# Folding the adjacency matrix over neighbouring 1024-column blocks instead of over its two halves

## The chip, the cores and the metric

The kernel runs on one core of a Trainium2 chip. The core has a TensorE (PE), a VectorE (DVE), a ScalarE (ACT), a GpSimd (POOL) and a SyncE (SP), and 16 DMA engines that all transfers share. The metric is device time in microseconds of one execution; the kernel before has a median of 1272.74 us over three runs (1272.05 to 1274.66).

## The reference

For x (8192 x 512) and adj (8192 x 8192, float32, sparse: about nine positive entries in a row, the diagonal always one of them):

```python
h = maximum(layernorm(x), 0)
mask = adj > 0
head = mask / maximum(sqrt(sum(mask * mask, -1)), 1e-12)
inc = adj + head                      # head is one value per row, at its nonzeros
out = x + (inc @ h) / sum(inc, -1)
```

## The kernel before, in words

The product is not done densely. For each row the kernel finds the nonzero entries and their columns, gathers those rows of h, and sums them with weights.

**Layer norm.** Sixteen chunks of 512 rows of x are loaded (L376), normed by DVE and ACT, and stored to a scratch tensor h in HBM (L380). A lane (partition) holds four rows in a run, so each lane's part of such a transfer is one run of 8 KB. ACT waits for the constants that POOL sets up (L466 to L491, one instruction after the other, each waited for) before its first piece of work (L732).

**Tiles.** There are 64 tiles of 128 rows, tile t being row t % 4 of each lane's four rows of chunk t // 4. The matrix rows of a tile are 4 MB. They come in four chunks of 1 MB (`load_chunk`, L382 to L391, queue of SP) into one of two buffers, `A[:, t % 2]`. A chunk j holds 1024 columns of the left half of the matrix and 1024 of the right half, the first beginning at 1024 j, the second at 4096 + 1024 j. In HBM these are two runs of 4 KB per lane, 16 KB apart; in SBUF they lie side by side, 8 KB.

**Fold.** For tiles 0 to 60 (`FOLDED` = 61) `fold` (L767) computes right * 2^100 + left into one row of 1024 words, on DVE. The entry tells by its size from which side it came. MAX8 (L794) and FIND_INDEX8 (L798) then take the eight greatest words and their places: 32 candidates in a row from four chunks. Where both sides have an entry in one column of a fold, or a chunk has over eight entries, the row is "bad". `check` on ACT (L564 to L575, four passes over 2048 words for each tile) and the list in `count_bad` (L1022) find such rows; up to 128 of them are done again in an extra tile, the batch (number 64), with no fold. In the matrix of the reference's inputs 51 rows of tiles 0 to 60 are bad with the fold over halves and 49 with the fold over neighbours (counted in that matrix; both are under 128, so the dense loop behind the batch, L433, is not entered). Tiles 61 to 63 and the batch are "wide": eight parts of 1024 columns, MAX8 and FIND_INDEX8 on each, no fold.

**Gather and product.** The two greatest of each chunk are a row's own entries, 8 slots; the rest spill, and the tile's spilled entries share 3 x 128 places (4 x 128 in the wide tiles). POOL gathers h rows of 2 KB with indirect DMAs, eight and three in a tile (`gather_own` L499, `gather_spill` L507); ACT builds diagonal matrices of the weights, and PE multiplies and sums them (L1326, L1337). Empty places name no row, so they move no data.

**Order.** Each engine has its order of work written out, in periods. In period t DVE does the four folds of tile t with the small work of tiles t - 1, t - 2 and t - 3 between them. SP, in period t, issues chunks 0 and 1 of tile t + 2, the store of tile t - 4 (L400, waits for ACT's copy), for t >= 16 the load of x for the residual (L396, waits for `own_done`, PE's own product of tile t - 2), and then chunks 2 and 3. A chunk's load waits until tile t has been checked by ACT and folded by DVE, and, if the diagonal of the tile lies in it (`diag_chunk`), until the diagonal has been read. So a chunk is asked for nearly two periods before it is folded.

**Names that the change touches.** `diag_half` and `diag_chunk` (L208, L211), `part` (L250), `load_chunk` (L391), the constants `base_own` and `base_spill` (L485, L487), `part_columns` to `part_places` (L801 to L818), `columns_any` (L862) and `count_bad` (L1028 to L1037).

Of the kernel before, what the change touches and what calls it, by code (L numbers as in the profile page):

```python
# [4 lines left out]
P = 128  # L5


def add_graph_layer(nc, x, adj, out):
# [14 lines left out]
    CHUNKS = 4  # L23
# [46 lines left out]
    adj_h = adj.rearrange("(c p j) (h n) -> c j p h n", p=P, j=ROWS, h=2)  # L70
# [3 lines left out]
    with ctx:  # L74
# [76 lines left out]
        right_diag = sb("right_diagonal_sign", [P, FOLDED - TILES // 2], fp32)  # L151
# [56 lines left out]
        def diag_half(t):  # L208
            return t // ROWS * P * ROWS // HALF

        def diag_chunk(t):  # L211
            return t // ROWS * P * ROWS % HALF // CW
# [36 lines left out]

        def part(i):  # L250
            return i % 2 * CHUNKS + i // 2
# [110 lines left out]
        def turn(t):  # L362
            return t // 2 + 1
# [8 lines left out]
        def _(sp):  # L372
# [9 lines left out]
            def load_chunk(t, j):  # L382
                if t >= 2:
                    sp.wait_ge(checked, 4 * (t - 2) + 2 * (j // 2) + 2)
                    if wide(t - 2):
                        sp.wait_ge(idx_found, searched(t - 2) + 2 * j + 2)
                    else:
                        sp.wait_ge(folded, CHUNKS * (t - 2) + j + 1)
                        if j == diag_chunk(t - 2):
                            sp.wait_ge(diag_read, t - 1)  # L390
                sp.dma_start(chunk(t % 2, j), adj_h[t // ROWS, t % ROWS, :, :, CW * j:CW * (j + 1)]).then_inc(adj_loaded[t % 2][j], 16)  # L391
# [58 lines left out]
        def _(pool):  # L450
# [19 lines left out]
            step(nc.gpsimd.memset(on_diag[:, FOLDED:BATCH + 1], 0.0))  # L470
            step(nc.gpsimd.memset(ones[:], 1.0))
# [13 lines left out]
            count_up(base_own[:, 0], [[0, 2], [CW, CHUNKS]], int(SKIP), 0)  # L485
            count_up(base_own[:, 1], [[CW, PARTS]], int(SKIP), 0)
            count_up(base_spill[:], [[0, 6], [-CW, CHUNKS]], 0, 0)  # L487
# [260 lines left out]
        def _(dve):  # L748
# [52 lines left out]
            def part_columns(t, i):  # L801
                if t == BATCH:
                    return A[:, 0, CW * part(i):CW * (part(i) + 1)]
                return chunk(t % 2, part(i) % CHUNKS)[:, part(i) // CHUNKS]

            def part_values(t, i):
                if t == BATCH:
                    dve.wait_ge(batch_adj, 16)
                else:
                    dve.wait_ge(adj_loaded[t % 2][part(i) % CHUNKS], 16 * turn(t))  # L810
                e = slice(8 * part(i), 8 * part(i) + 8)
                nc.vector.max(out=cv[:, t % 2, e], in_=part_columns(t, i)).then_inc(vals_found, 1)  # L812

            def part_places(t, i):
                dve.wait_ge(vals_found, searched(t) + i + 1)
                e = slice(8 * part(i), 8 * part(i) + 8)
                nc.vector.max_index(out=ci[:, t % 2, e], in_max=cv[:, t % 2, e],  # L817
                                    in_values=part_columns(t, i)).then_inc(idx_found, 1)  # L818
# [43 lines left out]
            def columns_any(t):  # L862
                dve.wait_ge(halves_told, t + 1)
                dve.wait_ge(idx_found, searched(t) + searches(t))
                nc.vector.scalar_tensor_tensor(out=ranked(cola[:], t), in0=ranked(ge[:], t), scalar=float(HALF),
# [156 lines left out]
            def count_bad():  # L1022
# [5 lines left out]
                on_right = slice(TILES // 2, FOLDED)  # L1028
                step(nc.vector.tensor_scalar(right_diag[:], on_diag[:, on_right], LEAST, None, ALU.is_ge))
                step(nc.vector.tensor_tensor(well[:], cnt_all[:, every], right_all[:, every], ALU.subtract))  # L1030
                step(nc.vector.tensor_tensor(well[:, on_right], well[:, on_right], right_diag[:], ALU.subtract))
# [4 lines left out]
                step(nc.vector.scalar_tensor_tensor(out=z_right[:, on_right], in0=right_diag[:], scalar=ZERO,  # L1036
                                                    in1=z_right[:, on_right], op0=ALU.mult, op1=ALU.add))  # L1037
# [415 lines left out]
```

## Time and profile before

| | |
|---|---|
| median of the runs | 1272.74 us (1272.05 to 1274.66) |
| profiled execution, span | 1276.7 us |
| DMA packets, MB | 148207, 471.00 |
| queue of SP (q1): packets, MB, share of 16 engines | 90368, 331.38, 66.3% |
| queue of POOL (q0): packets, MB, share of 16 engines | 57744, 138.64, 29.7% |
| adjacency chunks of 1 MB | 256 |

The span goes from the first to the last instruction of one profiled execution; its time is 4.0 us above the median of the runs, and no other time of that execution is given. A share of 16 engines is the time that packets took over 16 times the stretch; it can pass 100% a little, since packets overlap. "Remote" as a releaser means that the profile does not know it, and "issue" that the engine waited for nothing that the profile shows.

### The profile page before, as it was taken

Reading aid. Unit: us, or ns where it says so; the run is one execution under the profiler, and the core shown is the slowest. Engines: PE = TensorE matmul, PEld = TensorE weight load, DVE = VectorE, ACT = ScalarE, POOL = GpSimd, SP = SyncE. Lnnn points to the kernel's source line nnn. Section 1 sums busy time; section 2 is a strip of 40 time slices with the busy share of each in tenths; the row PEclk is TensorE's granted clock in tenths of the full one; section 3 lists DMA queues with packets and bytes.
Section 4 is the critical chain, followed back from the end, with each engine's and each line's share of the span. In section 5 each row is a group of like instructions: output and inputs, shape, how many; then the busy total and the mean of one; then the engine's idle time right before and its main releaser. Section 6 shows DMA issues by size and latency. Waiting matters only on the chain.

```text
span 1276.7 us, 14660 instructions
## 1 busy us (share of the span) xinstructions
PE 959.0 (75%) x2680; PEld 478.1 (37%) x2682; DVE 1189.2 (93%) x2868; ACT 975.5 (76%) x1902; POOL 791.1 (62%) x748
## 2 busy tenths in 40 slices
PE   0003878888888878787988887978878888977677
PEld 0001434444444444443434443434444434433343
DVE  6679999998999999998999999999999999999961
ACT  6657787887887988786888877888877888884731
POOL 1003667676666777776766767777776776765562
PEclk9999899898988989899898989999989988987888
DMA  9999999999999999999999999999999999997532
GB/s 356 427 422 406 396 394 388 369 387 369 379 378 382 401 373 401 395 401 394 402 400 401 392 374 384 399 400 395 402 396 402 402 397 373 401 390 275 175 106 74
DMA packets 148207, 471.00 MB, mean 369 GB/s; under 512 B 24826, under 2 KB 24826, under 8 KB 143965
## 3 DMA queue, kind: packets, MB, share of 16 engines
q1 hardware_dynamic: 90368, 331.38, 66.3%
q0 software_dynamic: 57744, 138.64, 29.7%
q8 instruction: 25, 0.41, 0.1%
q14 instruction: 70, 0.57, 0.1%
HBM read 490.47 MB, written 33.82 MB: 411 GB/s over the span
## 4 chain that ended last, share of the span: by engine, by line
DVE 55%; issue 17%; DMA 11%; ACT 6%; PE 6%; another core or an unknown queue 2%; SPq 1%; POOL 0%; DVEq 0%; ACTq 0%; POOLq 0%
DVE cand_word L794 17%; DVE folded L772 16%; DMA adj_tile<-in_adj_dram 8%; DVE cand_index L798 6%; DMA gathered_rows<-in_x_dram 3%; PE acc L1326 3%; DVE cand_index L817 2%; DVE cand_word L812 2%; ACT junk L573 2%; ACT adj_tile L560 2%; ACT diag L636 1%; PE acc L1337 1%; DVE diagonal_alone L779 1%; DVE entry L961 1%
## 5 line engine op out<-in xcount | busy, mean ns | idle before, releaser
L494 POOL DMA_INDIRECT gathered_rows<-h_scratch,slot_column x520 | 559.9, 1077 | 263.1 <-issue 158.0
L573 ACT ACTIVATE junk<-adj_tile,zero_unit 128x2048 bf16<-128x2048 f32 x256 | 510.0, 1998 | 48.3 <-issue 27.5
L1326 PE MATMUL acc<-gathered_rows,diag 128*128 128x512 f32 x1040 | 489.6, 622 | 21.4 <-DMA gathered_rows<-h_scratch,slot_column 18.2
L494 POOL DMA_INDIRECT gathered_rows<-h_scratch,spill_column x198 | 223.1, 1127 | 195.0 <-ACT spill_column L619 135.2
L794 DVE MAX8 cand_word<-folded 128x8 f32<-128x1024 f32 x244 | 298.2, 1222 | 5.9 <-remote 1.3
L772 DVE SCALAR_TENSOR_TENSOR folded<-adj_tile 128x1024 f32<-128x1024 f32 x244 | 296.1, 1214 | 7.7 <-DMA adj_tile<-in_adj_dram 5.6
L1326 PEld LDWEIGHTS acc<-gathered_rows,diag 128*128 128x128 f32 x1040 | 203.8, 204 | 263.4 <-issue 262.6
L798 DVE FIND_INDEX8 cand_index<-cand_word,folded 128x8 uint32<-128x1024 f32 x244 | 297.3, 1219 | 0.0
L1337 PE MATMUL acc<-gathered_rows,spill_matrix 128*128 128x512 f32 x396 | 186.8, 609 | 46.0 <-DMA gathered_rows<-h_scratch,spill_column 42.4
L636 ACT ACTIVATE diag<-ident,weights_and_payload 128x128 f32<-128x128 f32 x581 | 176.2, 388 | 16.0 <-issue 6.5
L1337 PEld LDWEIGHTS acc<-gathered_rows,spill_matrix 128*128 128x128 f32 x396 | 72.8, 192 | 154.8 <-issue 154.6
L1320 PE MATMUL acc<-own_row,diag 128*128 128x512 f32 x122 | 78.0, 726 | 68.6 <-ACT own_row L646 60.6
L1276 PE MATMUL poff<-spill_rank,lanes_before 128*128 128x1 f32 x130 | 22.7, 244 | 119.4 <-DVE spill_rank L859 116.8
L1299 PE MATMUL pbrought<-weights_and_payload,owner 128*128 128x72 f32 (+1 forms) x384 | 73.2, 340 | 30.8 <-DVE weights_and_payload L919 16.2
L1276 PEld LDWEIGHTS poff<-spill_rank,lanes_before 128*128 128x128 f32 x130 | 27.8, 226 | 163.5 <-issue 140.0
L611 ACT ACTIVATE owner<-powner,last_lane_half 128x384 f32<-128x384 f32 (+1 forms) x65 | 37.4, 575 | 58.1 <-remote 44.2
L1305 PE MATMUL pturned<-ident,owner 128*128 128x128 f32 x396 | 78.2, 350 | 0.6
L1299 PEld LDWEIGHTS pbrought<-weights_and_payload,owner 128*128 128x128 f32 x384 | 63.6, 243 | 33.2 <-issue 20.7
L1305 PEld LDWEIGHTS pturned<-ident,owner 128*128 128x128 f32 x396 | 67.4, 250 | 3.3 <-ACT spill_matrix L627 1.4
L646 ACT ACTIVATE own_row<-x_residual,ln_bias,ln_rstd 128x512 f32<-128x512 f32 x45 | 36.1, 802 | 38.0 <-remote 37.5
L1320 PEld LDWEIGHTS acc<-own_row,diag 128*128 128x128 f32 x122 | 23.6, 216 | 108.2 <-issue 91.8
L627 ACT ACTIVATE spill_matrix<-pturned,entry 128x128 f32<-128x128 f32 x198 | 57.1, 361 | 1.1 <-PE acc L1337 1.1
(151 smaller groups left out, 880.1 us busy)
## 6 DMA issues: line engine op xcount, KB each, us to landing
adj_tile<-in_adj_dram SPq DMA_DIRECT2D x256, 1024.0 KB
h_scratch<-adj_tile SPq DMA_DIRECT2D x16, 1024.0 KB, 10.6
out_dram<-out_tile SPq DMA_DIRECT2D x64, 256.0 KB
gathered_rows<-in_x_dram SPq DMA_DIRECT2D x12, 1024.0 KB, 12.6
x_residual<-in_x_dram SPq DMA_DIRECT2D x48, 256.0 KB
gathered_rows<-h_scratch,slot_column POOLq DMA_INDIRECT x520
x_held<-in_x_dram SPq DMA_DIRECT2D x4, 1024.0 KB, 7.9
gathered_rows<-h_scratch,spill_column POOLq DMA_INDIRECT x198, 3.5
```

The source lines that it names most:

```text
L494: nc.gpsimd.indirect_dma_start(out=into, out_offset=None, in_=h[:, :], in_offset=bass.IndirectOffsetOnAxis(ap=column, axis=0), bounds_chec ...
L573: nc.scalar.activation(junk[:, n % 2].rearrange("p (j c) -> p j c", j=2), both[:, :, half], ACT.Relu, bias=zero_unit[:], scale=-UP, accum_ ...
L627: last = nc.scalar.activation(W[:, t % 2, g], pturned[:, g * P:(g + 1) * P], ACT.Copy, scale=entry[:, t % 2, g, 0:1])
L636: last = nc.scalar.activation(diag[:, t % 2, s], ident[:], ACT.Copy, scale=wpay[:, t % 2, s:s + 1])
L772: nc.vector.scalar_tensor_tensor(out=F[:, j % 2], in0=a[:, 1], scalar=UP, in1=a[:, 0], op0=ALU.mult, op1=ALU.add).then_inc(folded, 1)
L794: nc.vector.max(out=cv[:, t % 2, 8 * j:8 * j + 8], in_=F[:, j % 2]).then_inc(vals_found, 1)
L798: nc.vector.max_index(out=ci[:, t % 2, 8 * j:8 * j + 8], in_max=cv[:, t % 2, 8 * j:8 * j + 8], in_values=F[:, j % 2]).then_inc(idx_found, 1)
L1299: last = nc.tensor.matmul(bank[:, c:c + 3 * n], owner[:, g * P:(g + 1) * P], wpay[:, t % 2, 1 + OWN:1 + OWN + 3 * n], start=True, stop=True)
L1305: last = nc.tensor.matmul(pturned[:, g * P:(g + 1) * P], owner[:, g * P:(g + 1) * P], ident[:], start=True, stop=True)
L1320: nc.tensor.matmul(acc[t % 3][:], diag[:, t % 2, 0], again[:], start=False, stop=False)
L1326: last = nc.tensor.matmul(acc[t % 3][:], diag[:, t % 2, 1 + s], slot(t % 2, s), start=False, stop=False)
L1337: last = nc.tensor.matmul(acc[t % 3][:], W[:, t % 2, g], slot(t % 2, OWN + g), start=False, stop=(g == groups(t) - 1))
```

## The change

A chunk is now 2048 columns in a row: columns 2048 j to 2048 j + 2047, of which the right 1024 are folded onto the left 1024. The load of a lane is one run of 8 KB. Bytes, chunks, folds, and the layout in SBUF within a chunk (left, right) are the same. The rest follows from that: which chunk and which side hold the diagonal, the columns' bases, and the wide tiles' parts, which now stand in order of the columns. Since the diagonal now is on the right side in every second group of eight tiles and not in tiles 32 to 60, POOL sets up a row of marks, `on_right`, with two more memsets, and `count_bad` works with all 61 tiles where it took 29.

```diff
-    adj_h = adj.rearrange("(c p j) (h n) -> c j p h n", p=P, j=ROWS, h=2)
+    adj_t = adj.rearrange("(c p j) n -> c j p n", p=P, j=ROWS)
...
         def diag_half(t):
-            return t // ROWS * P * ROWS // HALF
+            return t // ROWS * P * ROWS % (2 * CW) // CW
         def diag_chunk(t):
-            return t // ROWS * P * ROWS % HALF // CW
+            return t // ROWS * P * ROWS // (2 * CW)
...
-                sp.dma_start(chunk(t % 2, j), adj_h[t // ROWS, t % ROWS, :, :, CW * j:CW * (j + 1)]).then_inc(adj_loaded[t % 2][j], 16)
+                sp.dma_start(A[:, t % 2, 2 * CW * j:2 * CW * (j + 1)],
+                             adj_t[t // ROWS, t % ROWS, :, 2 * CW * j:2 * CW * (j + 1)]).then_inc(adj_loaded[t % 2][j], 16)
...
+            step(nc.gpsimd.memset(on_right[:], 0.0))
+            step(nc.gpsimd.memset(on_right[:].rearrange("p (c h k) -> p c h k", h=2, k=CW // P)[:, :, 1], 1.0))
...
-            count_up(base_own[:, 0], [[0, 2], [CW, CHUNKS]], int(SKIP), 0)
+            count_up(base_own[:, 0], [[0, 2], [2 * CW, CHUNKS]], int(SKIP), 0)
...
             def part_columns(t, i):
-                if t == BATCH:
-                    return A[:, 0, CW * part(i):CW * (part(i) + 1)]
-                return chunk(t % 2, part(i) % CHUNKS)[:, part(i) // CHUNKS]
+                return A[:, t % 2, CW * i:CW * (i + 1)]
...
-                nc.vector.scalar_tensor_tensor(out=ranked(cola[:], t), in0=ranked(ge[:], t), scalar=float(HALF),
+                nc.vector.scalar_tensor_tensor(out=ranked(cola[:], t), in0=ranked(ge[:], t), scalar=float(CW),
...
-                step(nc.vector.tensor_scalar(right_diag[:], on_diag[:, on_right], LEAST, None, ALU.is_ge))
+                step(nc.vector.scalar_tensor_tensor(out=bad_rank[:], in0=on_diag[:, every], scalar=LEAST,
+                                                    in1=on_right[:, every], op0=ALU.is_ge, op1=ALU.mult))
...
-                step(nc.vector.tensor_tensor(well[:, on_right], well[:, on_right], right_diag[:], ALU.subtract))
+                step(nc.vector.tensor_tensor(well[:], well[:], bad_rank[:], ALU.subtract))
...
-                step(nc.vector.scalar_tensor_tensor(out=z_right[:, on_right], in0=right_diag[:], scalar=ZERO,
-                                                    in1=z_right[:, on_right], op0=ALU.mult, op1=ALU.add))
+                step(nc.vector.scalar_tensor_tensor(out=z_right[:], in0=bad_rank[:], scalar=ZERO,
+                                                    in1=z_right[:], op0=ALU.mult, op1=ALU.add))
```

## Rows read from the trace of the kernel before

**Rows 1.** The page: busy time by engine, and the DMA engines' tenths in 40 slices.

```profile
PE 959.0 (75%) x2680; PEld 478.1 (37%) x2682; DVE 1189.2 (93%) x2868; ACT 975.5 (76%) x1902; POOL 791.1 (62%) x748
...
DMA  9999999999999999999999999999999999997532
```

**Rows 2.** Windows: PE, PEld, DVE, ACT, POOL busy, clock, DMA share, GB/s.

```profile
0.00:20.00 20.00, 0.00 (x0) 0.00 (x0) 12.62 (x43) 12.20 (x19) 5.02 (x27) 1.00 0.85 313
100.00:200.00 100.00, 73.34 (x192) 36.87 (x193) 99.59 (x231) 81.39 (x152) 60.87 (x56) 0.93 1.02 395
...
1000.00:1100.00 100.00, 85.77 (x238) 42.98 (x239) 97.24 (x230) 79.79 (x157) 71.48 (x64) 0.90 1.02 391
```

**Rows 3.** Timeline of VectorE, two folds of a first chunk (start, us, instruction).

```profile
198.87 1.22 DVE L772 SCALAR_TENSOR_TENSOR folded<-adj_tile 128x1024 f32<-128x1024 f32 x1
...
215.87 1.22 DVE L772 SCALAR_TENSOR_TENSOR folded<-adj_tile 128x1024 f32<-128x1024 f32 x1
```

**Rows 4.** Waits of VectorE to 98.5 us (waited for: total us, times, longest).

```profile
DVE folded L772 <- DMA adj_tile<-in_adj_dram: 3.3, 3, 1.2
```

**Rows 5.** Waits of VectorE, 98.5 to 900 us.

```profile
DVE entry_value L833 <- remote: 3.3, 2, 1.7
...
DVE cand_word L794 <- remote: 1.3, 1, 1.3
```

**Rows 6.** Waits of VectorE, 900 to 1110 us.

```profile
DVE folded L772 <- DMA adj_tile<-in_adj_dram: 2.2, 4, 0.8
DVE folded L772 <- issue: 2.1, 2, 1.4
```

**Rows 7.** DMA queues, 20 to 60 us (packets, MB, share of 16 engines).

```profile
DMA packets 2353, 17.12 MB, mean 428 GB/s; under 512 B 263, under 2 KB 263, under 8 KB 263
...
q1 hardware_dynamic: 2351, 17.11, 101.3%
```

**Rows 8.** DMA queues, 84 to 96 us.

```profile
DMA packets 1039, 5.07 MB, mean 422 GB/s; under 512 B 77, under 2 KB 77, under 8 KB 764
...
q1 hardware_dynamic: 1039, 5.07, 101.5%
```

**Rows 9.** DMA queues, 400 to 900 us.

```profile
q1 hardware_dynamic: 39509, 135.50, 69.6%
q0 software_dynamic: 25431, 60.68, 32.2%
```

**Rows 10.** Chain that ended last (start us, us, what).

```profile
82.49 15.74 DMA adj_tile<-in_adj_dram
...
1011.32 2.21 SPq L396
...
1021.02 25.63 DMA adj_tile<-in_adj_dram
```

**Rows 11.** Chain that ended last, the first 10 us.

```profile
2.37 0.11 POOL ones L471
2.52 0.11 POOL zero_unit L472
...
7.53 0.21 ACT place_plus_half L732
...
9.70 2.93 ACT adj_tile L560 x4
```

**Rows 12.** Timeline of VectorE, list of bad rows.

```profile
1159.51 0.19 DVE L1031 TENSOR_TENSOR tests_passed<-tests_passed,right_diagonal_sign 128x29 f32<-128x29 f32 x1
1159.73 0.22 DVE L1032 SCALAR_TENSOR_TENSOR zeros_left<-tests_passed,zeros_left 128x61 f32<-128x61 f32 x1
```

**Rows 13.** Waits of TensorE, whole span.

```profile
PE acc L1337 <- DMA gathered_rows<-h_scratch,spill_column: 42.4, 29, 2.9
PE acc L1326 <- DMA gathered_rows<-h_scratch,slot_column: 18.2, 18, 2.3
```

**Rows 14.** Timeline of GpSimd, one gather.

```profile
214.52 1.00 POOL L494 DMA_INDIRECT gathered_rows<-h_scratch,slot_column  x1 [0.30 <-issue]
```

More of the change, by code:

```diff
@@ L150, in add_graph_layer @@
         well = sb("tests_passed", [P, FOLDED], fp32)
-        right_diag = sb("right_diagonal_sign", [P, FOLDED - TILES // 2], fp32)
+        on_right = sb("diagonal_on_right", [P, TILES], fp32)
         bad = sb("bad_rows", [P, FOLDED], fp32)
@@ L247, in searched @@
             return CHUNKS * min(t, FOLDED) + PARTS * max(t - FOLDED, 0)
-        def part(i):
-            return i % 2 * CHUNKS + i // 2
         def paid(t, k):
@@ L484, in _ @@
             count_up(placed[:], [[P, EXTRA]], 1, 1)
-            count_up(base_own[:, 0], [[0, 2], [CW, CHUNKS]], int(SKIP), 0)
+            count_up(base_own[:, 0], [[0, 2], [2 * CW, CHUNKS]], int(SKIP), 0)
             count_up(base_own[:, 1], [[CW, PARTS]], int(SKIP), 0)
-            count_up(base_spill[:], [[0, 6], [-CW, CHUNKS]], 0, 0)
+            count_up(base_spill[:], [[0, 6], [-2 * CW, CHUNKS]], 0, 0)
             count_up(b_base_spill[:], [[0, 7], [-CW, PARTS]], 0, 0)
@@ L809, in part_values @@
                 else:
-                    dve.wait_ge(adj_loaded[t % 2][part(i) % CHUNKS], 16 * turn(t))
-                e = slice(8 * part(i), 8 * part(i) + 8)
+                    dve.wait_ge(adj_loaded[t % 2][i // 2], 16 * turn(t))
+                e = slice(8 * i, 8 * i + 8)
                 nc.vector.max(out=cv[:, t % 2, e], in_=part_columns(t, i)).then_inc(vals_found, 1)
@@ L815, in part_places @@
                 dve.wait_ge(vals_found, searched(t) + i + 1)
-                e = slice(8 * part(i), 8 * part(i) + 8)
+                e = slice(8 * i, 8 * i + 8)
                 nc.vector.max_index(out=ci[:, t % 2, e], in_max=cv[:, t % 2, e],
@@ L1026, in count_bad @@
                 step(nc.vector.tensor_tensor(z_right[:], q_all[:, every, 1], q_all[:, every, 3], ALU.add))
-                on_right = slice(TILES // 2, FOLDED)
-                step(nc.vector.tensor_scalar(right_diag[:], on_diag[:, on_right], LEAST, None, ALU.is_ge))
+                step(nc.vector.scalar_tensor_tensor(out=bad_rank[:], in0=on_diag[:, every], scalar=LEAST,
+                                                    in1=on_right[:, every], op0=ALU.is_ge, op1=ALU.mult))
                 step(nc.vector.tensor_tensor(well[:], cnt_all[:, every], right_all[:, every], ALU.subtract))
-                step(nc.vector.tensor_tensor(well[:, on_right], well[:, on_right], right_diag[:], ALU.subtract))
+                step(nc.vector.tensor_tensor(well[:], well[:], bad_rank[:], ALU.subtract))
                 step(nc.vector.scalar_tensor_tensor(out=z_left[:], in0=well[:], scalar=ZERO, in1=z_left[:],
```

## The prediction

> **What bounds the kernel now.** I read the busy shares first, then the windows, the waits of VectorE, the DMA queues, and last the chain. VectorE is busy 93% of the span, ahead of ScalarE with 76% and TensorE with 75% [rows 1]. The windows sharpen that: from 100 to 200 us VectorE works 99.59 of 100 us, from 1000 to 1100 us 97.24 [rows 2]. The reader should see in the same rows that the DMA share is 1.02 in both, where 1.013 is what a stretch of nothing but queued transfers shows [rows 7]. So two resources are full. A tile costs VectorE 17.00 us (from 198.87 to 215.87, the first folds of two tiles in a row) [rows 3], and the DMA engines need about as long for the same tile. Which is the slower one is told by who waits. Ahead of the fold VectorE waits 3.3 us until 98.5 us, when the pipeline fills [rows 4]; from 900 to 1110 us 2.2 + 2.1 = 4.3 us [rows 6]; and never between: what it waits for there is no transfer [rows 5]. The second row of group 6 has "issue" as releaser; but the fold has only two conditions, the load and a search two chunks back on its own engine, so I take it as a late load too. The transfers are falling behind: a chunk landed 15.74 us after its issue at 82 us, and 25.63 us after it at 1021 us, where the chain runs through such transfers [rows 10]. VectorE is the bound of the first 50 tiles, the DMA engines by a hair that of the last ten folded ones.
>
> **The load, the part that matters.** All 64 tiles x 4 chunks x 128 lanes x 2 runs = 65536 runs of 4 KB become 32768 of 8 KB. What a run costs comes from two stretches. From 20 to 60 us there are 2351 - 263 = 2088 packets of 8 KB on the queue of SP in 1.013 x 40 x 16 = 648.3 us of engine time: 0.3105 us each, the 263 small ones counted at nothing [rows 7]; it also shows that a run of 8 KB goes as one packet. From 84 to 96 us there are 1039 - 764 = 275 packets of 8 KB and 764 - 77 = 687 of 4 KB in 1.015 x 12 x 16 = 194.9 us: (194.9 - 275 x 0.3105) / 687 = 0.1594 us for one of 4 KB [rows 8]. Two of those are 0.3188, so a joined run saves 0.0083 us of one DMA engine. Over 16 engines that is 128 x 0.0083 / 16 = 0.066 us for a chunk, 0.27 us for a tile, 17.0 us over the run. The rounding of the shares leaves about 0.0005 us on the 0.0083, or 1 us on the 17.
>
> Most of the 17 us buys nothing, because VectorE needs its 17.00 us for a tile whatever the transfers do. In the middle it only makes loads land earlier. What it can take from the time is the wait ahead of folds:
> - From 900 to 1110 us: by tile 52 the transfers have 52 x 0.27 = 14 us more in hand, over three times the 4.3 us that is lost there. I take all of it: -4.3 us. Bounds: 0 (the loads are late for another reason, below) and -4.3.
> - To 98.5 us: here the DMA engines are the bound, and stay it. Five chunks stand ahead of the fold at 98.26 us, 5 x 0.066 = 0.33: -0.3 us.
> - After 1110 us no fold or search waits for a load. The drain is a chain of gathers and products; it keeps its length and moves with VectorE.
>
> By the Trainium skill ("DMA: Bandwidth & Descriptors", section "Why small descriptors are slow (HBM only)") the fixed part of a packet is about 3 cycles, on a fabric that the same page puts at 850 MHz. An estimate from that page is 3.5 ns a packet, 32768 x 3.5 / 16 = 7.2 us over the run, where the rows gave 17.0. Even so the 52 tiles would bring 5.8 us, over the 4.3 us needed, and the sum would be the same but for 0.2 us at the start.
>
> **The small edits.** Two memsets on POOL stand in the chain of constants that ScalarE waits for before the layer norm. Such a step takes 2.52 - 2.37 = 0.15 us with its wait, and the chain of the first 10 us runs over POOL and into ScalarE's L732 with nothing between [rows 11]; the DMA engines have room then, the share is 0.85 [rows 2]: +0.3 us. The second memset is strided; nothing here shows one, and I bound it by 0 and by one more step of 0.15. In `count_bad` three operations grow from 29 to 61 elements. Of 29 they take 0.18 to 0.19, of 61 0.22 [rows 12]: 3 x 0.04, +0.1 us, on VectorE's path. The tiles whose diagonal gates a load are 16, 16, 16 and 13 for chunks 0 to 3, as before; only which ones they are differs. Diagonal reads, searches and `columns_any` have the same shapes. ScalarE's checks read the same words of SBUF.
>
> **Sum.** -4.3 - 0.3 + 0.3 + 0.1 = -4.2 us on the span of 1276.7 us: 1272.5. The profiled execution is 4.0 us above the median of the runs, and I carry the difference over: 1272.7 - 4.2 = 1268.5 us, 0.33% faster.
>
> **Rivals.**
> 1. *The loads are late because SP asks late.* SP issues chunks 2 and 3 behind a load of x that waits for TensorE's own product; the chain passes exactly there, SP L396 at 1011.32 us and then a transfer of 25.63 us [rows 10]. If the order of SP's queue decides, the 4.3 us stays and the time is 1272.7 - 0.3 + 0.4 = 1272.8 us. Against it: the long part of that chain is the transfer, which is 10 us longer than at 82 us. To this belongs also that the loads are cut in pieces of 4 KB all the same; against that stand the 8 KB packets of [rows 7]. 27%.
> 2. *More is won.* VectorE lost 3.3 + 1.3 us on waits with no known releaser between 98 and 900 us [rows 5], while transfers went on and caught up. If those belong to the profiled execution, the runs had 4.6 us more lateness of transfers, and all of it goes: 1268.5 - 4.6 = 1263.9 us. For it: the DMA share has no hole. Against: nothing shows the two kinds of execution side by side. 12%.
> 3. *The gathers are starved; slower.* The DMA engines serve two queues that are both never empty. A tile's gathers move 60.68 MB / (500 / 17.0) = 2.06 MB [rows 9], 504 pieces of 4 KB if rows go in pairs, 31.5 for each engine, 2.9 for each of eleven gathers. If the engine takes turns by packets, a gather takes 2.9 x (0.159 + 0.159) = 0.92 us now, under the 1.00 + 0.30 us at which POOL issues them [rows 14]; behind 8 KB packets it takes 2.9 x (0.159 + 0.3105) = 1.36 us, over it. The eight own gathers then end 0.44 + 8 x 0.06 = 0.9 us later, the three spilled ones 0.6 us: 1.5 us a tile for TensorE, which waits for gathers already, 60.6 us in all [rows 13]. It is idle (100 - 85.77) x 17 / 100 = 2.4 us a tile [rows 2], so this is hidden unless it stands in the chain gather, own product, load of x, chunks 2 and 3 [rows 10]. From the point where it does, say the eight tiles 52 to 59, it costs 8 x 1.5 = 12 us and the 4.3 is not won: 1272.8 + 12 = 1285 us. 13%.
>
> That taking of turns is what the Trainium skill states ("DMA: Bandwidth & Descriptors", section "Queues, rings and completion order"): an engine goes round its queues packet by packet. It is the rule that speaks against this change. No row here shows an engine's turns; what rival 3 counts with are the durations of the rows.
>
> **How the numbers follow.** The forecast has 48%, rival 1 27%, rival 2 12%, rival 3 13%. A measurement of this kernel tells 0.2%, 2.5 us, from no change. The forecast is beyond that by 1.7 us, rival 2 well beyond, rival 1 within: faster 60%, within 27%, slower 13%. The range takes in rivals 1 and 2 with a margin and leaves most of rival 3 out: 1261 to 1275 us. The forecast's own range is 1267 to 1271.
>
> **What would show it.** Packets on the queue of SP fall by 32768 to about 57600 with the same MB, and its share of the engines by 17.0 / 1276.7 = 1.3 points. The fold's waits from 900 to 1110 us are gone, those to 98.5 us still about 3. Chunks land some 10 us or more sooner after their issue late in the run. VectorE's tile stays at 17.00 us. TensorE's waits for gathers stay near 60 us; if they double and folds wait again, rival 3 holds. If the packets fall and the waits at the end remain, it is rival 1, and the step that failed is the one that gives the transfers' rate the lateness.

## The result: 0.4% slower, with late gathers in the place of late loads

The changed kernel takes 1278.38 us (median of 4 runs, 1276.44 to 1279.47), the kernel before 1273.40 us beside it (4 runs, 1272.05 to 1274.66): a ratio of 1.0042, 95% interval 1.0027 to 1.0057. The forecast was 1268.5 us, with a range to 1275. The profiled execution has a span of 1274.6 us; it belongs to the fastest of the four runs, so its waits are on the small side, while the profiled execution of the kernel before lies 4.0 us above its median. This pair of profiles shows what changed in kind and not the loss itself: from the first fold to the last, VectorE stands still for 11.0 us in the changed kernel and for 15.7 us in the kernel before (stops over 0.25 us, added up from the two traces). A run counts in a ratio if it is within 1.5% of the fastest of its kernel; that left out one of six runs of `small_owner_first` (1623 us) and two of six of `split_lanes`, and no other.

First the page of the changed kernel: span, busy shares, the DMA totals with the two queues (packets, MB, share of 16 engines), and the chain that ended last by engine.

```profile
span 1274.6 us, 14664 instructions
...
PE 939.1 (74%) x2682; PEld 451.2 (35%) x2682; DVE 1189.8 (93%) x2868; ACT 972.5 (76%) x1902; POOL 803.8 (63%) x750
...
DMA packets 115439, 470.98 MB, mean 370 GB/s; under 512 B 24824, under 2 KB 24824, under 8 KB 78431
...
q1 hardware_dynamic: 57600, 331.38, 65.3%
q0 software_dynamic: 57744, 138.62, 29.7%
...
DMA 23%; issue 21%; DVE 21%; PE 15%; POOL 9%; ACT 7%; another core or an unknown queue 1%; POOLq 1%; ACTq 0%; SPq 0%; DVEq 0%
```

VectorE's busy time is what it was [rows 1]. The queue of SP has 57600 packets, 32768 fewer, for the same 331.38 MB. The chain is another one: DMA, TensorE and GpSimd make up 23 + 15 + 9 = 47% of it and VectorE 21%, where before the three made up 11 + 6 + 0 = 17% and VectorE 55%.

From 84 to 96 us all loads are now 8 KB (columns as in [rows 8]):

```profile
DMA packets 704, 5.11 MB, mean 426 GB/s; under 512 B 80, under 2 KB 80, under 8 KB 80
...
q1 hardware_dynamic: 704, 5.11, 101.0%
```

1.010 x 12 x 16 = 193.9 us for 704 - 80 = 624 packets is 0.3108 us each, the price that [rows 7] gave.

VectorE's waits over the whole span (total us, times, longest), against [rows 4 to 6]:

```profile
DVE weights_and_payload L917 <- ACT half_minus_offset L597: 7.1, 9, 2.5
...
DVE folded L772 <- DMA adj_tile<-in_adj_dram: 3.6, 3, 1.3
DVE weights_and_payload L917 <- issue: 3.5, 7, 1.7
```

The fold's wait for loads is 3.6 us in all, and the three stops behind it are those of the filling, until 99 us; the 4.3 us of [rows 6] are gone. In their place stand 7.1 + 3.5 = 10.6 us ahead of L917, the payload of places, which needs ScalarE's `half_minus_offset`. Of these, 8.0 us lie between 98.5 and 1110 us, where the kernel before has none; the rest comes behind 1110 us, where it has 2.6 us too. TensorE's waits for gathered rows, against [rows 13]:

```profile
PE acc L1324 <- DMA gathered_rows<-h_scratch,slot_column: 61.2, 33, 3.8
PE acc L1335 <- DMA gathered_rows<-h_scratch,spill_column: 56.9, 31, 3.4
```

These are 118.1 us, where they were 60.6. With the stops that have no releaser shown, TensorE is idle ahead of these two products for 176.9 us, where it was 67.2. That second measure is the one used below to compare kernels, since profiles differ in how many stops they can name. And ScalarE's copy of the owners waits. It did so in the kernel before too, 57.7 us in all, of which 2.9 us are put down to TensorE by name and the rest so:

```profile
ACT owner L611 <- remote: 44.2, 17, 8.7
ACT owner L611 <- issue: 10.6, 8, 2.9
```

In the changed kernel it is 152.1 us in all, most of it by name:

```profile
ACT owner L611 <- PE powner L1282: 123.8, 42, 8.5
```

What ties the three together is seen in the chain that ended last, here from 297 us on (start, us, what):

```profile
297.55 9.09 DMA gathered_rows<-h_scratch,spill_column
...
306.78 5.46 PE acc L1335 x6
312.24 0.33 PE powner L1282
...
313.08 0.20 ACT spill_column L619
...
314.04 0.33 POOL gathered_rows L494
...
316.70 7.43 DMA gathered_rows<-h_scratch,spill_column
...
325.02 4.27 PE acc L1335 x6
329.29 0.44 PE powner L1282
...
333.81 7.53 DMA gathered_rows<-h_scratch,spill_column
```

Read it as a loop. The spilled rows of one tile land 9.09 us after the step ahead of them, TensorE makes their product (L1335), only then finds the owners of a younger tile (L1282), ScalarE copies these and, next in its order, converts a third tile's spill columns (L619), GpSimd issues its gathers (L494), and the loop is at the landing of the next tile's rows: 316.70 to 333.81 is 17.11 us a turn, the turn before it (297.55 to 316.70) 19.15. VectorE's tile takes 17.00 [rows 3]. The loop has become as long as VectorE's own or longer, and VectorE, which needs one turn of it for each tile, stands ahead of L917. The kernel before has the same loop in its code, but none of the 195 longest pieces of its chain is a transfer of gathered rows of h.

The constants' chain at the start, against [rows 11]:

```profile
7.95 0.21 ACT place_plus_half L732
...
10.12 2.23 ACT adj_tile L560 x3
```

L732 starts at 7.95 us where it started at 7.53, and the first layer norm at 10.12 where it was 9.70: the two memsets cost 0.4 us.

### The profile page after: what moved, and what is told of

Read it like the earlier page. It is cut to its first block, busy times and chain, and to the rows that moved or that the text cites. A ratio compares the mean times of both kernels' runs of the same rounds, so it can differ in the third digit from the quotient of the medians.

```text
span 1274.6 us, 14664 instructions
## 1 busy us (share of the span) xinstructions
PE 939.1 (74%) x2682; PEld 451.2 (35%) x2682; DVE 1189.8 (93%) x2868; ACT 972.5 (76%) x1902; POOL 803.8 (63%) x750
## 3 DMA queue, kind: packets, MB, share of 16 engines
q1 hardware_dynamic: 57600, 331.38, 65.3%
## 4 chain that ended last, share of the span: by engine, by line
DMA 23%; issue 21%; DVE 21%; PE 15%; POOL 9%; ACT 7%; another core or an unknown queue 1%; POOLq 1%; ACTq 0%; SPq 0%; DVEq 0%
DMA gathered_rows<-h_scratch,spill_column 13%; POOL gathered_rows L494 9%; PE acc L1335 8%; DMA gathered_rows<-h_scratch,slot_column 6%; PE acc L1324 5%; DVE cand_word L794 5%; DVE folded L772 5%; DMA gathered_rows<-in_x_dram 3%; ACT junk L573 3%; DVE cand_index L815 2%; DVE cand_word L810 2%; DVE cand_index L798 2%; ACT adj_tile L560 2%; DMA adj_tile<-in_adj_dram 1%; ACT diag L636 1%
## 5 line engine op out<-in xcount | busy, mean ns | idle before, releaser
L494 POOL DMA_INDIRECT gathered_rows<-h_scratch,slot_column x520 | 578.9, 1113 | 262.9 <-issue 157.8
L1324 PE MATMUL acc<-gathered_rows,diag 128*128 128x512 f32 x1040 | 501.1, 629 | 80.4 <-DMA gathered_rows<-h_scratch,slot_column 61.2
L494 POOL DMA_INDIRECT gathered_rows<-h_scratch,spill_column x198 | 216.6, 1094 | 180.1 <-ACT spill_column L619 126.0
L1335 PE MATMUL acc<-gathered_rows,spill_matrix 128*128 128x512 f32 x396 | 207.7, 667 | 96.9 <-DMA gathered_rows<-h_scratch,spill_column 56.9
L1335 PEld LDWEIGHTS acc<-gathered_rows,spill_matrix 128*128 128x128 f32 x396 | 78.0, 209 | 221.0 <-issue 221.0
L611 ACT ACTIVATE owner<-powner,last_lane_half 128x384 f32<-128x384 f32 (+1 forms) x65 | 38.0, 584 | 152.1 <-PE powner L1282 123.8
L1297 PE MATMUL pbrought<-weights_and_payload,owner 128*128 128x72 f32 (+1 forms) x384 | 60.4, 296 | 16.7 <-DVE weights_and_payload L917 15.4
L1318 PE MATMUL acc<-own_row,diag 128*128 128x512 f32 x122 | 63.5, 602 | 8.1 <-ACT own_row L646 7.4
L1303 PE MATMUL pturned<-ident,owner 128*128 128x128 f32 x396 | 62.4, 298 | 0.3
L627 ACT ACTIVATE spill_matrix<-pturned,entry 128x128 f32<-128x128 f32 x198 | 57.7, 367 | 3.4 <-PE acc L1335 3.4
L1297 PEld LDWEIGHTS pbrought<-weights_and_payload,owner 128*128 128x128 f32 x384 | 51.8, 202 | 17.9 <-issue 17.1
L1303 PEld LDWEIGHTS pturned<-ident,owner 128*128 128x128 f32 x396 | 53.9, 206 | 1.0 <-ACT spill_matrix L627 0.7
L573 ACT ACTIVATION_READ_ACCUMULATOR junk<-adj_tile,zero_unit 128x1 f32 x256 | 50.9, 199 | 0.0
## 6 DMA issues: line engine op xcount, KB each, us to landing
gathered_rows<-in_x_dram SPq DMA_DIRECT2D x12, 1024.0 KB, 12.6
```

The costliest lines, as they stand in the source:

```text
L494: nc.gpsimd.indirect_dma_start(out=into, out_offset=None, in_=h[:, :], in_offset=bass.IndirectOffsetOnAxis(ap=column, axis=0), bounds_chec ...
L573: nc.scalar.activation(junk[:, n % 2].rearrange("p (j c) -> p j c", j=2), both[:, :, half], ACT.Relu, bias=zero_unit[:], scale=-UP, accum_ ...
L627: last = nc.scalar.activation(W[:, t % 2, g], pturned[:, g * P:(g + 1) * P], ACT.Copy, scale=entry[:, t % 2, g, 0:1])
L1297: last = nc.tensor.matmul(bank[:, c:c + 3 * n], owner[:, g * P:(g + 1) * P], wpay[:, t % 2, 1 + OWN:1 + OWN + 3 * n], start=True, stop=True)
L1303: last = nc.tensor.matmul(pturned[:, g * P:(g + 1) * P], owner[:, g * P:(g + 1) * P], ident[:], start=True, stop=True)
L1318: nc.tensor.matmul(acc[t % 3][:], diag[:, t % 2, 0], again[:], start=False, stop=False)
```

## The experiments

Eighteen kernels ran in five groups, each group on one chip. The first chip is that of the result; experiments 1 and 2 ran on the second, experiment 3 and two kernels of experiment 4 on the third, the other four of experiment 4 on the fourth, experiment 5 on the fifth and experiment 6 on a sixth. Every ratio is to the kernel before, run beside it on the same chip; that kernel itself took 1269 to 1284 us on them, so only ratios compare across chips.

**1. The changed columns with the load written as two runs.**

```diff
-                sp.dma_start(A[:, t % 2, 2 * CW * j:2 * CW * (j + 1)],
-                             adj_t[t // ROWS, t % ROWS, :, 2 * CW * j:2 * CW * (j + 1)])...
+                sp.dma_start(chunk(t % 2, j), adj_t[t // ROWS, t % ROWS, :, j])...   # p h c on both sides
```

> The changed kernel, with the load of a chunk written as two runs of 1024 columns per lane (left, right) in place of one of 2048: the same columns, folds, edits and bytes. Theory A (8 KB packets take the DMA engines' turns from the gathers): if the two runs stay two packets of 4 KB (q1 back at 90368 packets), TensorE's waits for gathered rows fall from 118 us to about 61 as in the kernel before, VectorE's waits ahead of the payload of places (10.6 us) fall under 2, late fold waits of some us return, and the time is 1273 to 1275 us. Theory B (the columns' new places in HBM or the small edits cost it): it stays at 1277 to 1279 us. If the packets stay at 57600, the runs are joined on the way and the run says nothing but noise: 1278.

It failed as an experiment: 57600 packets on the queue of SP, so the two neighbouring runs were joined into one. It is the changed kernel a second time, on another chip: ratio 1.0026 (1.0001 to 1.0051), TensorE's waits for gathers 133.3 us, VectorE 13.9 us ahead of the payload (12.2 us of it between 98.5 and 1110 us). There the runs scattered over 1.3%.

**2. One step of VectorE later, in either kernel, and the kernel before again.**

```diff
                 fold(t, 0)
-                if pay:
-                    pay_places(q)
...
                 find_places(t, 0)
                 if small:
                     counts(p)
+                if pay:
+                    pay_places(q)
```

> The changed kernel with one VectorE step moved: the payload of places of tile t-2 (which waits for ScalarE's half_minus_offset) comes some 4 us later in the period, behind the counts of tile t-1 in place of right behind the first fold. Packets and gathers as in the changed kernel. Theory A with its chain (late spill gather, TensorE's spill product, owner, ScalarE's offset, VectorE's payload): VectorE's 10.6 us of waits there go, TensorE's waits for gathers stay near 118 us, time 1278.4 - 8 to 10.6 = 1268 to 1271 us. Theory B (something else slows the runs, and the waits are only seen beside it): 1277 to 1279 us.

> Control: the same move of one VectorE step in the kernel before. There the step waited for nothing in the middle of the span, so theory A expects no change within 1 us: 1272.5 to 1274.5 us. If the move itself is worth something apart from the late gathers, it is faster than 1271.

> The kernel before, unchanged, for a second profile and the noise of the comparison: ratio 1.000 within 0.001. It tells whether the 4.3 us of late loads from 900 to 1110 us and the 8 us of waits of VectorE without a known releaser are in every execution. Theory A: late loads 3 to 9 us again, the waits without a releaser in other places or fewer. If the late loads are absent here, the prediction's gain had nothing to take.

Measured: 1.0016 (0.9990 to 1.0042), 0.9994 (0.9967 to 1.0021), 0.9999 (0.9976 to 1.0021). The first is a miss: the forecast was 1268 to 1271 us against 1273.4, and 1.0016 cannot be told from the 1.0026 of the unmoved kernel on that chip. The wait did not go, it moved to the next step that needs ScalarE (VectorE's waits of that kernel):

```profile
DVE head L891 <- ACT root L589: 18.2, 8, 3.0
```

So it is not one step that is placed badly; ScalarE as a whole is late, and the place of the payload is not the cause. `before_again` told something else: in its profile the fold waits for no load between 100 and 1110 us. The 4.3 us of [rows 6] that the forecast counted on is not in every execution of the kernel before.

**3. The link that TensorE's order makes.**

```diff
-                if end:
-                    product_spill(f)
                 if pay:
                     find_owner(q)
+                if end:
+                    product_spill(f)
```

> The changed kernel with one step of TensorE's order moved: the product that finds the owners of tile t-2 now ahead of the spill product of tile t-4, which waits for gathered rows. Theory A with the chain late spill gather, spill product, owner, ScalarE: ScalarE's waits of the owner copy for TensorE (80 to 124 us) fall under 40 us, VectorE's waits ahead of the payload (10 to 14 us) mostly go, ratio to before 0.995 to 1.000. If the chain passes only through what is behind the spill product as well (residual, offsets), the waits move to the offset and the root and the ratio stays at 1.002 to 1.004. Theory B: no change, 1.002 to 1.004.

> Control: the same move in the kernel before, where the owner copy waits some 44 us (releaser not known) in all and VectorE hardly for it. Theory A: no change, ratio 0.998 to 1.001. If it gains as much as in the changed kernel, the move is worth something by itself and says nothing on the gathers.

Measured: 0.9978 (0.9962 to 0.9993) in the changed kernel, 0.9989 (0.9979 to 0.9999) in the kernel before. In the first, VectorE's waits ahead of the payload and TensorE's for gathers:

```profile
DVE weights_and_payload L917 <- issue: 1.8, 1, 1.8
```

```profile
PE acc L1335 <- DMA gathered_rows<-h_scratch,spill_column: 43.6, 24, 3.0
PE acc L1324 <- DMA gathered_rows<-h_scratch,slot_column: 35.6, 25, 2.9
```

ScalarE's wait for the owners is no longer among its large ones. TensorE still waits for the gathers, 79.2 us by this name and 92.7 us more ahead of the same two products with no releaser shown (49.0 + 43.7); but their lateness no longer reaches ScalarE and VectorE. That closes the loop from the other side: with its link out, the changed kernel is 0.2% under before, where it was 0.3 to 0.4% over it on three chips (the unmoved one did not run on this third chip). The control gained 0.1%, so some 0.1 of the 0.5 points may belong to the move by itself.

**4. Packets of 4 KB and of 8 KB with as many DMAs.** Two kernels with the changed columns. The first loads a chunk by two DMAs of 1024 columns, the second by one of 2048 and a small one of 16 lanes x 8 bytes into a tile of its own. Waits for a chunk count 32 in both.

```diff
+                for i in (2 * j, 2 * j + 1):      # split_columns
+                    sp.dma_start(A[:, t % 2, CW * i:CW * (i + 1)],
+                                 adj_t[t // ROWS, t % ROWS, :, CW * i:CW * (i + 1)])...
...
+                # split_small, behind the load of 2048 columns
+                sp.dma_start(dump[:, t % 2, j], adj_t[t // ROWS, t % ROWS, 0:16, 2 * j:2 * j + 2])...
```

> The changed kernel, columns and small edits as there, but each chunk loaded by two DMAs, one for each 1024 columns, so that its packets are 4 KB again (q1: 32768 more packets than the changed kernel, and 4096 more small ones). To be read against split_small, which has as many DMAs with 8 KB packets. Theory A (packet size starves the gathers): TensorE's waits for gathered rows fall to about 60 us as in the kernel before (118 to 133 us with 8 KB), ScalarE's waits of the owner copy for TensorE fall from 100 and more to under 50, VectorE does not wait ahead of the payload of places, and it is 3 to 8 us faster than split_small. Theory B (the place of the columns in HBM, or the small edits): waits and time as split_small within 1.5 us.

> The changed kernel with 8 KB packets and a second DMA of 16 lanes x 8 bytes behind each chunk into a tile of its own, which only makes the number of DMAs and of their end packets that of split_columns. Theory A: gathers late as in the changed kernel, TensorE waits 110 to 135 us for them, time at or up to 3 us above the changed kernel (ratio to before 1.003 to 1.007). Theory B expects the same, but then also for split_columns.

> The changed kernel itself, beside the two split kernels on one chip. So far the ratio to before was 1.0042 (first chip) and 1.0026 (second chip, as near_two_runs), and the split kernel with 8 KB packets had 0.9965 on a third. Theory A1 (the small DMA behind each chunk of split_small lets the gathers in and so removes the cost): 1.002 to 1.005 here, split_small 0.995 to 0.998. Theory C (it is the chip: the changed kernel is slower on some and faster on others, since gain and cost are both some us): the changed kernel and split_small within 0.0015 of each other, wherever that is.

> split_small again (8 KB packets, a second DMA of 8 bytes x 16 lanes behind each chunk). Theory A1: 0.995 to 0.998 and under the changed kernel by 0.4% or more. Theory C: as the changed kernel within 0.15%. TensorE's waits for gathers 105 to 130 us by both.

> split_columns again (two DMAs per chunk, 4 KB packets). TensorE's waits for gathers under 60 us by every theory that holds the packet size for their cause. Time: 0.998 to 1.000 of before if packet size alone sets it, since it has the packets of before; slower than 1.002 if the columns' place or the small edits cost what the changed kernel loses.

> split_small with TensorE's owner product ahead of the spill product (as in after_owner_first). If the wait of that product for late gathers is what is left of the cost, it is at or under split_small: 0.994 to 0.997, the candidate for the fastest version. If split_small has no such cost left, equal within 0.1%.

| kernel | packets | chip | ratio to before (95%) | TensorE idle ahead of the two products of gathered rows | VectorE: loads after the filling / payload |
|---|---|---|---|---|---|
| split_columns | 4 KB | 3rd | 0.9987 (0.9975 to 0.9998) | 36.8 us | 4.8 / 0.4 us |
| columns_again | 4 KB | 4th | 0.9986 (0.9977 to 0.9995) | 40.8 us | 5.4 / 0 us |
| after_again | 8 KB | 4th | 1.0039 (1.0022 to 1.0056) | 188.6 us | 0 / 16.3 us |
| split_small | 8 KB, a small DMA | 3rd | 0.9965 (0.9951 to 0.9978) | 148.9 us | 0 / 1.9 us |
| small_again | 8 KB, a small DMA | 4th | 0.9939 (0.9926 to 0.9952) | 136.4 us | 0 / 0 us |
| small_owner_first | same, TensorE's order of 3. | 4th | 0.9936 (0.9923 to 0.9949) | 134.7 us | 1.3 / 0 us |

The three that matter stand on one chip. Waits of VectorE and TensorE of the changed kernel there:

```profile
DVE weights_and_payload L917 <- ACT half_minus_offset L597: 16.3, 13, 3.4
...
DVE folded L772 <- DMA adj_tile<-in_adj_dram: 3.3, 3, 1.1
```

```profile
PE acc L1335 <- DMA gathered_rows<-h_scratch,spill_column: 101.2, 52, 3.6
PE acc L1324 <- DMA gathered_rows<-h_scratch,slot_column: 87.4, 51, 5.3
```

of the one with the small DMA:

```profile
DVE folded L774 <- DMA dump<-in_adj_dram: 3.3, 3, 1.1
```

```profile
PE acc L1337 <- DMA gathered_rows<-h_scratch,spill_column: 92.8, 54, 3.1
PE acc L1326 <- DMA gathered_rows<-h_scratch,slot_column: 43.6, 40, 2.6
```

and of the one with 4 KB packets:

```profile
DVE folded L773 <- DMA adj_tile<-in_adj_dram: 8.7, 11, 1.6
```

```profile
PE acc L1336 <- DMA gathered_rows<-h_scratch,spill_column: 37.1, 31, 2.6
```

The payload's 1.9 us of split_small lie behind 1110 us, as in the kernel before. One expectation was missed outright: split_small was to be no faster than the changed kernel and 3 to 8 us slower than split_columns, and it came out 2.8 us faster than split_columns (1268.5 and 1271.3 us). What these kernels say is this. The columns' place is out: with 4 KB packets the same columns and small edits are 0.1% under before. Out too is the claim that larger packets cost in any case, since split_small and small_again have them. 8 KB packets take the late loads away (8.7 - 3.3 = 5.4 us of fold waits with 4 KB, none with 8 KB), and they make gathers late; the changed kernel shows both, and with the small DMA the first stays and the payload's waits are gone. TensorE's clock does not explain the loss: on the fourth chip 0.925 of full speed was granted to columns_again, 0.944 to after_again and 0.966 to small_again. `small_owner_first` adds nothing that could be measured (median 1260.5 us). The kernel with the small DMA is the fastest that ran, 0.6% under before and 1.0% under the changed kernel on that chip.

**5. What the small DMA does.**

> split_small with the small DMA ahead of its chunk in SP's queue and not behind it. Theory T (the small DMA breaks the run of 8 KB packets, so gathers get in and the loss goes): as split_small, 0.993 to 0.997 of before. Theory W (what helps is that the chunk is declared loaded later, by a DMA behind it, which shifts ScalarE's check): near the changed kernel, 1.002 to 1.005.

> split_small with two small DMAs behind each chunk. Theory T: TensorE's waits for gathers under those of split_small (113 and 136 us), 0.992 to 0.997. If the small DMAs only cost (256 x 2 x 16 more packets on the queue, some 0.3 us of engine time each 256), it is 1 to 3 us slower than split_small and still under before.

> The kernel before (halves, 4 KB packets) with the same small DMA behind each chunk. Theory T: its gathers get in already (TensorE waits some 60 us), so nothing is won: 0.998 to 1.002. If the small DMA is worth 8 us in itself, by the order of the queue and not by packet size, it is 0.993 to 0.996 here too, and the changed kernel's loss is not told by packet size alone. VectorE's waits without a known releaser (8 us in the profile of before) then go.

> The changed columns, each chunk in two DMAs of 64 lanes, 8 KB packets, no small DMA. Packets on q1: 32768 + 24832 + 4096. Theory T by turns of small packets: only the end packets of the DMAs double (16 more a chunk), so it lies between the changed kernel and split_small, 0.997 to 1.003. Theory P (it is the number of DMAs on SP's queue, not their packets, that spaces the 8 KB bursts): as split_small, 0.993 to 0.997. If 64 lanes load the DMA engines unevenly, folds wait for loads and it is slower than 1.005.

Measured, on the fifth chip: ahead of its chunk 0.9959 (0.9943 to 0.9975); twice 0.9949 (0.9934 to 0.9964); in the kernel before 1.0024 (1.0013 to 1.0036); two DMAs of 64 lanes 1.5681. That it is the later wait on the chunk is out, since the small DMA helps from ahead as well. That it is worth something by itself is out too: with 4 KB packets it costs 0.2%. It helps only where the chunks come in 8 KB packets. Neither the changed kernel nor split_small ran on this chip, so these ratios are set against theirs on other chips. When a gather lands can be read from the packet records of GpSimd's queue, where each gather ends with 16 packets of 4 bytes. From the start of the instruction of a tile's last spilled gather to the end of the sixteenth of them, median over the 55 to 57 tiles between 100 and 1100 us:

| packets of the chunks | from start to landing, us |
|---|---|
| 4 KB | before 6.1, before_again 6.1, before_late_pay 6.2, before_owner_first 6.1, split_columns 5.9, columns_again 5.8 |
| 4 KB and a small DMA | before_small 5.8 |
| 8 KB | after 7.8, near_two_runs 7.8, after_late_pay 7.8, after_owner_first 8.2, after_again 7.6 |
| 8 KB and a small DMA | split_small 7.2, small_again 7.1, small_owner_first 7.2, small_ahead 7.1 |
| 8 KB and two small DMAs | small_twice 6.5 |

So 8 KB packets make this gather land 1.4 to 2.4 us later. The small DMA takes about 0.5 us of that back and a second one 0.6 us more, though it brings no time that could be measured (0.9949 against 0.9959): VectorE's waits for the payload were gone with the first. TensorE's idle time ahead of the two products goes the same way: 32 to 67 us, 172 to 189, 135 to 149, and 80.9 in small_twice. An estimate of the turns fits the order. A chunk gives each DMA engine 8 packets of 8 KB (0.31 us by [rows 7]) and one of 4 bytes, and each small DMA adds two small ones, so a mean turn of SP's queue is 8 x 0.31 / 9 = 0.28 us, 0.23 with one small DMA and 0.19 with two, and 0.15 with 16 packets of 4 KB. `after_owner_first`, with the latest landing of all, is 0.2% under before: the lateness costs only through what waits behind it.

split_lanes was to give the same number of DMAs without small packets. It tells nothing of the gathers, because it broke the loads (DMA totals and queue of SP, 400 to 900 us):

```profile
DMA packets 31004, 118.03 MB, mean 236 GB/s; under 512 B 7702, under 2 KB 7702, under 8 KB 22066
...
q1 hardware_dynamic: 15321, 80.65, 70.3%
```

118.03 MB in 500 us, 236 GB/s, where 4 KB packets over 128 lanes moved 393 (before) and 8 KB packets 396 (after). The 16 engines are busy all the same (70.3% and 32.1% of their time), since a packet takes longer: one of 8 KB 0.54 us in the mean, where it took 0.32 in the changed kernel.

**6. The disputed cost by itself.** Nothing but a stream of chunks, eight outstanding, and gathers of 128 rows one after the other; nothing of the reference is computed.

> A measurement of the disputed cost alone; nothing of the reference is computed, only chunks are loaded (128 of 1 MB, two runs of 4 KB a lane as in the kernel before, eight outstanding) and 96 gathers of 128 rows are made one after the other, each waited for. Theory T (turns by packets): a gather's 128 rows are 64 packets of 4 KB, 4 for each engine, each behind one 4 KB packet: 4 x (0.159 + 0.159) = 1.3 us of service beside a fixed part that is the same in both kernels.

> The same with chunks of 2048 columns in a row, one run of 8 KB a lane. Theory T: 4 x (0.159 + 0.309) = 1.9 us of service, so a gather lands 0.6 us or more later than in stream_far (up to twice that if a packet also waits at its first place in the queue). A theory by which the gathers' lateness comes from the kernel's order and not from the queue: no difference within 0.1 us. Load rate: 2 to 3% higher than in stream_far while both run.

Two gathers in a row in the stream of 4 KB packets (start, us, idle before), the totals from 50 to 300 us, and one of the later gathers, when the stream was over:

```profile
102.30 1.00 POOL L51 DMA_INDIRECT gathered_rows<-in_x_dram,column  x1 [6.09 <-DMA gathered_rows<-in_x_dram,column]
109.38 1.00 POOL L51 DMA_INDIRECT gathered_rows<-in_x_dram,column  x1 [6.08 <-DMA gathered_rows<-in_x_dram,column]
```

```profile
DMA packets 26855, 101.85 MB, mean 407 GB/s; under 512 B 1993, under 2 KB 1993, under 8 KB 26853
...
q1 hardware_dynamic: 23998, 92.48, 92.9%
```

```profile
402.80 1.00 POOL L51 DMA_INDIRECT gathered_rows<-in_x_dram,column  x1 [3.25 <-DMA gathered_rows<-in_x_dram,column]
```

and in the stream of 8 KB packets:

```profile
103.73 1.00 POOL L51 DMA_INDIRECT gathered_rows<-in_x_dram,column  x1 [6.84 <-DMA gathered_rows<-in_x_dram,column]
111.41 1.00 POOL L51 DMA_INDIRECT gathered_rows<-in_x_dram,column  x1 [6.69 <-DMA gathered_rows<-in_x_dram,column]
```

```profile
DMA packets 15789, 104.71 MB, mean 419 GB/s; under 512 B 1984, under 2 KB 1984, under 8 KB 4032
...
q1 hardware_dynamic: 13227, 96.30, 93.0%
```

From start to start the median is 7.08 us in the first (36 gathers, 20 to 280 us), 7.77 us in the second (33 gathers), and 4.18 us in both once the stream has ended. So a gather of 128 rows loses 0.69 us by the larger packets, against 4 x 0.150 = 0.60 from the turns.

The packet records of these two traces show the turns themselves. A gather is 64 packets of 4 KB. From the start of the first to the end of the last, 1.43 us go by in the one stream and 1.99 us in the other (medians), and in that time 78 and 68 packets of the stream are started: about one for each packet of the gather, whatever its size. That is 0.56 of the 0.69 us. From the start of the instruction to the first packet it is 4.2 us in both.

The other way, all transfers together move 419 GB/s and not 407, 2.9% more. The loads alone move 96.30 MB and not 92.48, 4.1% more, while the gathers, each of which is waited for, move 8.39 MB and not 9.35. The two prices of [rows 7, 8] say 0.3188 / 0.3105, 2.7%.

## Why the prediction was wrong

**The load's price** was about right. The 0.3105 us for 8 KB came back as 0.3108 from 84 to 96 us of the changed kernel; beside gathers both kinds take longer, 0.164 us for 4 KB and 0.315 for 8 KB in the two streams (means of the packet records), so that joining two saves 12.6 ns there and not 8.3. q1's share fell by 1.0 point of the 1.3 that were named.

**The gain of 4.3 us** was the right mechanism: with 8 KB packets folds waited 0 to 1.4 us for loads after the filling, in ten profiles (split_lanes left out), with 4 KB 0.1 to 7.9 us in seven. Its size depends on the execution, and in the second profile of the kernel before it was 0.1 us. The fastest kernel with TensorE's order as it was, small_again, is 8.6 us under before on its chip. Against columns_again, which has 4 KB packets, its profile is 7.4 us shorter: 5.4 us are the waits for loads, 1.6 us lie behind the last fold; the remaining 0.4 us and the difference between columns_again and before (2.4 us of the medians) were not taken apart.

**The small edits** were named at 0.4 us together; the start shows 0.4 for the memsets, where 0.3 was taken and the strided one bounded at 0.15 more.

**The step that failed** is the one that made rival 3 a case of 13%: "It is idle ... 2.4 us a tile, so this is hidden unless it stands in the chain gather, own product, load of x, chunks 2 and 3". By it the sum of the forecast has no term for late gathers, and "TensorE's waits for gathers stay near 60 us". They were 118.1 us, and VectorE lost 8.0 us by them in the middle of the first profile and 16.3 us on the fourth chip. The cost of a turn was well sized: 0.44 us for 2.9 packets against 0.69 us measured for 4. What it does to a gather in the kernel was too small: 0.6 us for the spilled ones of a tile, against a landing of the last of them 1.7 us later after its start (6.1 and 7.8 us). The mechanism that failed is the cover: an engine's idle time was used as cover where the question was what waits in order behind the late work. TensorE's idle 2.4 us a tile did not hide it, because the owners of another tile stood behind the spill product, and ScalarE's next steps behind the owners. And only one chain was looked through, that of SP's queue, since it was in the chain of the kernel before; the loop over `find_owner`, `copy_owner` and `spill_columns` could be read from the order of the code, with each engine's place in it. SP's own chain did get later, from 900 to 1110 us its load of x waited 35.4 us for TensorE against 24.1 before (13.3 of it with no releaser shown), and yet no fold waited. Taking out the loop's one link (experiment 3) or shortening the landing (experiment 4) left no wait of the payload before 1110 us.

**The size** of the loss came out smaller than the rival's 12 us and spread over the span: 1278.38 - 1273.40 = 5.0 us in the medians. The payload's waits are 8.0 us in the middle of the first profile and 16.3 on the fourth chip, less the late loads that were won; since loads and gathers pull in opposite directions, the sign of the sum hangs on both sizes.

**The rule on turns** from the Trainium skill ("DMA: Bandwidth & Descriptors", section "Queues, rings and completion order") was the one that spoke against the change, and the runs agree with it if one run is taken for a packet: 0.69 us measured against the 0.60 that turns by packets give from the rows, and about one stream packet started for each gather packet. The page's rule on the fixed part of a packet (section "Why small descriptors are slow (HBM only)"), 3.5 ns as an estimate from the page, is under the 8.3 ns of the rows and the 12.6 ns of the streams, and the measurements decide.

**Rival 2** held that the waits without a releaser go with lighter queues. They are absent from the profiles of the changed kernel and of small_again, but also from columns_again, with 4 KB packets, and present in before_again. What they are stays open.

## What to carry to other kernels

In these runs a larger packet was cheaper for its own queue and dearer for the one beside it, so where small transfers with a consumer in waiting share the engines with a bulk stream, price both: here 2.9% more moved in all against 0.7 us on each gather of 128 rows. Idle time of an engine is cover only for work that nothing waits behind in order; before a late transfer is called hidden, follow what its consumer's engine does next and who waits for that, round to the transfer's own issue. A loop of that kind shows no wait on the bounding engine until it becomes the bound: the payload of VectorE waited for nothing in the middle of the kernel before, while ScalarE, inside the loop, already waited 57.7 us for the owners.

## What was not expected

- Writing a load as two runs that lie side by side in both memories does not make two packets: the count stayed at 57600 (experiment 1).
- A DMA of 16 lanes x 8 bytes behind each 1 MB load made the kernel 1.0% faster than without it (small_again against after_again, one chip).
- Two DMAs of 64 lanes moved data at 236 GB/s where one of 128 lanes gave 396, with the engines as busy. Why was not tried.
- A gather of 128 rows took 4.18 us from start to start on idle DMA engines and 7.08 us beside a stream, and the turns are not why. By the packet records its 64 packets take 1.37 and 1.43 us; the first of them starts 1.70 and 4.23 us after the instruction. What goes on in those 2.5 us stays open.
